# Down product of the last mixture from three products of rounded halves, transposes in pairs, result stored by groups

## The reference

```python
x = x + jnp.tanh(g_xattn[0]) * _L0_xattn_ref(_layernorm(x, axis=-1), ...)
x = x + jnp.tanh(g_ffn[0]) * _L0_ffn_ref(_layernorm(x, axis=-1), ...)
x = x + jnp.tanh(g_xattn[1]) * _L1_xattn_ref(_layernorm(x, axis=-1), ...)
x = x + jnp.tanh(g_ffn[1]) * _L1_ffn_ref(_layernorm(x, axis=-1), L1_ffn_gate_weight,
                                         L1_ffn_gate_up_weights, L1_ffn_down_weights,
                                         L1_ffn_shared_gate_up, L1_ffn_shared_down)
return x
```

## Time and profile before

| | us |
|---|---|
| median of 3 runs | 1322.51 |
| the three runs | 1320.82, 1322.51, 1324.74 |
| the profiled execution, its own time | 1319.32 |
| span of its trace | 1317.6 |
| busy PE, PEld, DVE, ACT, POOL | 1034.8, 852.9, 686.0, 431.5, 278.8 |
| last mixture, first product L1977 to last residual | 1003.3 to 1309.5 |

### The profile page before, as it was taken

The page is one execution under the profiler, slowest core; times in us unless marked ns, Lnnn a source line. Parts: engine busy times, 40 slices in busy tenths (PEclk is TensorE's granted clock), DMA queues, the critical chain, the costliest instruction groups (busy, mean ns, idle before and its releaser), DMA issues. The chain is left out here.

```text
span 1317.6 us, 16309 instructions
## 1 busy us (share of the span) xinstructions
PE 1034.8 (79%) x5307; PEld 852.9 (65%) x5307; DVE 686.0 (52%) x1618; ACT 431.5 (33%) x792; POOL 278.8 (21%) x225
## 2 busy tenths in 40 slices
PE   5989989989866502766566468797989999999997
PEld 3867858768655302656565236464668989898996
DVE  6277576675659895222223497556575324233221
ACT  4555455464624200111111042424252232322321
POOL 0414214133000002788787111010100000000000
PEclk9999999999886755788887676868667999899999
DMA  7004000000000141888886530000000000000001
GB/s 270 3 0 139 1 1 1 0 1 1 1 0 20 40 132 38 174 179 176 173 174 114 186 119 1 2 0 0 0 0 1 1 0 0 0 0 0 0 1 64
DMA packets 58887, 66.33 MB, mean 50 GB/s; under 512 B 5021, under 2 KB 55639, under 8 KB 58071
## 3 DMA queue, kind: packets, MB, share of 16 engines
q1 hardware_dynamic: 45188, 46.45, 11.3%
q0 software_dynamic: 12288, 18.88, 8.2%
q10 hardware_dynamic: 1363, 0.37, 0.1%
HBM read 48.13 MB, written 17.56 MB: 50 GB/s over the span
## 5 line engine op out<-in xcount | busy, mean ns | idle before, releaser
L1977 PE MATMUL bank<-gu_hi,xnT_split 128*128 128x352 f32 x640 | 158.7, 328 | 0.0
L474 POOL TENSOR_TENSOR q_lo<-soft,q_hi 128x512 fp32r<-128x512 f32 x64 | 93.3, 1458 | 236.1 <-ACT soft L1326 236.0
L1977 PEld LDWEIGHTS bank<-gu_hi,xnT_split 128*128 128x128 f32 x640 | 112.6, 190 | 1.0 <-issue 0.7
L495 POOL DMA_INDIRECT acc<-y,dst_now x64 | 102.3, 1598 | 26.3 <-issue 19.5
L485 POOL DMA_INDIRECT xg<-table,src_now x64 | 64.1, 1001 | 202.9 <-DVE src_now L940 183.7
L1977 PE MATMUL bank<-gu_lo,xnT_split 128*128 128x352 f32 x320 | 103.7, 324 | 0.0
L1196 DVE SCALAR_TENSOR_TENSOR soft<-sg,combine_w,bank 128x176 f32<-128x176 f32 x160 | 56.5, 395 | 87.6 <-PE bank L1977 81.8
L1996 PE MATMUL bank<-dn,attnT 128*128 128x256 f32 x448 | 101.8, 385 | 0.0
L1996 PEld LDWEIGHTS bank<-dn,attnT 128*128 128x128 f32 x448 | 85.9, 195 | 11.4
L713 DVE COPY qT<-bank 128x512 f32<-128x512 f32 x64 | 44.2, 691 | 87.4 <-PE bank L1675 86.3
L1528 ACT ACTIVATE sg<-bank 128x352 f32<-128x352 f32 x80 | 37.2, 465 | 152.0 <-PE bank L1977 151.9
(11 more groups left out here) (265 smaller groups left out, 2155.5 us busy)
## 6 DMA issues: line engine op xcount, KB each, us to landing
w_gu<-in_L_ffn_w_gu SPq DMA_DIRECT2D x32, 352.0 KB
w_dn<-in_L_ffn_w_down SPq DMA_DIRECT2D x32, 176.0 KB
acc<-zeros SPq DMA_DIRECT2D x2, 2176.0 KB, 11.4
acc_rows<-acc SPq DMA_DIRECT2D x8, 512.0 KB, 5.0
gu<-in_L_gu SPq DMA_DIRECT2D x1, 3520.0 KB, 13.8
table<-xw SPq DMA_DIRECT2D x4, 640.0 KB
wo<-in_L_xattn_Wo SPq DMA_DIRECT2D x2, 1024.0 KB, 16.0
wq<-in_L_xattn_Wq SPq DMA_DIRECT2D x1, 2048.0 KB, 18.3
```

The costliest lines, as they stand in the source:

```text
L474: pool.tensor_tensor(q2_lo[:, h % 3, :], q2[h % 2], q2_hi[:, h % 3, :], ALU.subtract).then_inc(q2_split, 1)
L495: pool.indirect_dma_start(acc[e], bass.IndirectOffsetOnAxis(ap=dst_now[:, q, e:e + 1], axis=0), y[:, q, e, :], None, compute_op=ALU.add).t ...
L1977: mm = pe.matmul(b[:, 0:2 * F1], v[:, c, j * P:(j + 1) * P], w[:, c, p, o, :], start=(n == 0), stop=(n == len(terms) - 1))
```

## The change

- The down weights are split once, in the first group, behind tile 0's silu and products: ACT rounds `dn1` to `dn_hi`, DVE subtracts to `dn_lo`, which lies on `dn1`. For this the first group is written out ahead of a loop over the two next.
- The transposes leave `down` and become `turn(j, groups)`. For tiles 0, 1 and 2 of a group they stand in the gates_ups of the next tile, two banks ahead of its third pair and two ahead of its fifth. For tile 3 all four banks stand ahead of down(3).
- ACT copies a turned bank rounded to `actT_hi`, and doesn't free it; DVE subtracts (`split_products`) to `actT_lo` and frees it. The last 96 rows of the 14th chunk are an instruction of their own.
- `down` does three products of fp32r for each chunk: hi x hi, hi x lo, lo x hi.
- ACT's exponential for the routing stands ahead of the copies of tile 3. PE waits, before the front, for the last turned bank.
- SP stores `x` in four transfers, one as soon as a group's four residuals are done.

```diff
@@ -224,7 +224,12 @@
-        dn1 = sb("dn1", [P, FC, DIM])
+        loaded = ExitStack()
+        dn1 = sb("dn1", [P, FC, DIM], scope=loaded)
+        loaded.close()
+        dn_lo = sb("dn_lo", [P, FC, DIM], F32R)
+        actT_hi = sb("actT_hi", [P, FC, P], F32R)
+        actT_lo = sb("actT_lo", [P, FC, P], F32R)
@@ -246,9 +251,12 @@
-        k_blocks = sb("k_blocks", [P, 2, C, 8, SKV])
-        v_blocks = sb("v_blocks", [P, 2, 2, 8, 2, D1])
-        c1 = sb("c1", [P, 2, DIM])
+        context = ExitStack()
+        k_blocks = sb("k_blocks", [P, 2, C, 8, SKV], scope=context)
+        v_blocks = sb("v_blocks", [P, 2, 2, 8, 2, D1], scope=context)
+        c1 = sb("c1", [P, 2, DIM], scope=context)
+        context.close()
+        dn_hi = sb("dn_hi", [P, FC, DIM], F32R)
@@ -444,9 +454,10 @@
-            sp.wait_ge(x_done, 1)
-            sp.dma_start(out_d, x[:]).then_inc(stored, 16)
-            sp.wait_ge(stored, 16)
+            for i in range(NG):
+                sp.wait_ge(o_read, 2 + 3 * NT + G * (i + 1))
+                sp.dma_start(out_d[:, G * i:G * (i + 1), :], x[:, G * i:G * (i + 1), :]).then_inc(stored, 16)
+            sp.wait_ge(stored, 16 * NG)
@@ -1068,6 +1079,15 @@
+            LAST = W1 - (FC - 1) * P
...
+            def split_down():
+                dve.wait_ge(dn_rounded, 1)
+                dve.tensor_tensor(dn_lo[:, 0:FC - 1], dn1[:, 0:FC - 1], dn_hi[:, 0:FC - 1], ALU.subtract).then_inc(
+                    dn_split, 1)
+                dve.tensor_tensor(dn_lo[0:LAST, FC - 1], dn1[0:LAST, FC - 1], dn_hi[0:LAST, FC - 1],
+                                  ALU.subtract).then_inc(dn_split, 1)
@@ -1171,7 +1191,7 @@
-                dve.wait_ge(t_ring.free, T5 + TMF - 8 + TM * i)
+                dve.wait_ge(t_ring.free, T5 + TMF - 4 + TM * i)
@@ -1186,9 +1206,25 @@
-            def products(i, j):
+            def split_products(i, j, groups):
...
+                for g in groups:
+                    n = min(4, FC - 4 * g)
+                    dve.wait_ge(act_rounded, 16 * i + 4 * j + g + 1)
+                    b = tr.read(dve)
+                    whole = n if g < 3 else n - 1
+                    ins = dve.tensor_tensor(actT_lo[:, 4 * g:4 * g + whole, :], b[:, 0:whole * P].rearrange(
+                        "p (f t) -> p f t", f=whole), actT_hi[:, 4 * g:4 * g + whole, :], ALU.subtract)
+                    if whole < n:
+                        ins = dve.tensor_tensor(actT_lo[0:LAST, FC - 1, :], b[0:LAST, whole * P:n * P],
+                                                actT_hi[0:LAST, FC - 1, :], ALU.subtract)
+                    ins.then_inc(t_ring.free, 1)
...
+            def products(i, j, before=None):
...
+                    if before is not None and p in (2, 4):
+                        split_products(i, before, (0, 1) if p == 2 else (2, 3))
@@ -1199,26 +1235,33 @@
+            tr = t_ring.end()
...
             def mixture(i, last):
...
                 qr.at(Q5, QM, i)
+                tr.at(T5 + TMF, TM, i)
                 products(i, 0)
+                if i is first_mixture:
+                    split_down()
                 if not last:
                     row_stats(i + 1)
-                products(i, 1)
+                products(i, 1, 0)
                 if not last:
...
                     row_apply(i + 1)
-                products(i, 2)
+                products(i, 2, 1)
                 residual(3 * NG + i, 1, i, 3)
-                products(i, 3)
-                if not last:
+                products(i, 3, 2)
+                if not last:
+                    tr.skip(TMF)
                     split_xn(i + 1)
...
                 residual(3 * NG + i, 2, i, 3)
+                split_products(i, 3, range(4))
                 residual(3 * NG + i, 3, i, 3)
@@ -1229,10 +1272,11 @@
             dve.wait_ge(o_read, 2 + 3 * NT)
-            with dve.Fori(0, NG - 1) as i:
+            first_mixture = 0
+            mixture(0, False)
+            with dve.Fori(1, NG - 1) as i:
                 mixture(i, False)
             mixture(NG - 1, True)
-            dve.drain().then_inc(x_done, 1)
@@ -1520,35 +1564,46 @@
-                def silu(j):
+                def silu(j, before=None):
                     for p in range(5):
+                        if before is not None and p in (2, 4):
+                            act_out(before, (0, 1) if p == 2 else (2, 3))
                         b = sr.read(act)
...
-                def act_out(j):
-                    for g in range(4):
+                def round_down():
+                    act.activation(dn_hi[:, 0:FC - 1], dn1[:, 0:FC - 1], ACT.Copy)
+                    act.activation(dn_hi[0:LAST, FC - 1], dn1[0:LAST, FC - 1], ACT.Copy).then_inc(dn_rounded, 1)
...
+                def act_out(j, groups):
+                    for g in groups:
                         n = min(4, FC - 4 * g)
-                        act.activation(attn_flat[:, 4 * g:4 * g + n, :], tr.read(act)[:, 0:n * P].rearrange(
-                            "p (f t) -> p f t", f=n), ACT.Copy).then_inc(t_ring.free, 1)
+                        b = tr.read(act)
+                        whole = n if g < 3 else n - 1
+                        ins = act.activation(actT_hi[:, 4 * g:4 * g + whole, :], b[:, 0:whole * P].rearrange(
+                            "p (f t) -> p f t", f=whole), ACT.Copy)
+                        if whole < n:
+                            ins = act.activation(actT_hi[0:LAST, FC - 1, :], b[0:LAST, whole * P:n * P], ACT.Copy)
+                        ins.then_inc(act_rounded, 1)
...
                 silu(0)
-                silu(1)
-                act_out(0)
-                silu(2)
-                act_out(1)
-                silu(3)
+                if i is first_mixture:
+                    round_down()
+                silu(1, 0)
+                silu(2, 1)
+                silu(3, 2)
                 if not last:
                     mixture_front()
-                act_out(2)
-                if not last:
                     gate_exponential(i + 1)
-                act_out(3)
...
-            attn_flat = attnT[:].rearrange("p b f t -> p (b f) t")
+                act_out(3, range(4))
...
+            LAST = W1 - (FC - 1) * P
             gate_exponential(0)
-            with act.Fori(0, NG - 1) as i:
+            first_mixture = 0
+            mixture(0, False)
+            with act.Fori(1, NG - 1) as i:
                 mixture(i, False)
@@ -1966,8 +2021,10 @@
-                def gates_ups(j):
+                def gates_ups(j, before=None):
                     for p in range(5):
+                        if before is not None and p in (2, 4):
+                            turn(before, (0, 1) if p == 2 else (2, 3))
                         for o, (ring, end) in enumerate(((s_ring, sr), (q_ring, qr))):
@@ -1978,40 +2035,52 @@
-                def down(j):
+                def turn(j, groups):
...
                     pe.wait_ge(q_ring.free, Q5 + QM * i + 5 * (j + 1))
-                    for g in range(4):
+                    for g in groups:
                         b = tr.fill(pe)
...
                         mm.then_inc(t_ring.full, 1)
+                    turned[j] = tr.k
...
+                turned = {}
...
+                def down(j):
...
                     pe.wait_ge(o_read, G * (3 * NG + i) + j + 1)
...
                         if f % 4 == 0:
-                            tr.evacuated(pe, 4 - f // 4)
-                        mm = pe.matmul(o_banks[j % 2][:, 0:DIM], attn_flat[0:n, f, :], dn1[0:n, f, :],
-                                       start=(f == 0), stop=(f == FC - 1))
+                            tr.evacuated(pe, tr.k - turned[j] + 4 - f // 4)
+                        for k, (v, w) in enumerate(((actT_hi, dn_hi), (actT_hi, dn_lo), (actT_lo, dn_hi))):
+                            mm = pe.matmul(o_banks[j % 2][:, 0:DIM], v[0:n, f, :], w[0:n, f, :],
+                                           start=(f == 0 and k == 0), stop=(f == FC - 1 and k == 2))
                     mm.then_inc(o_full, 1)
...
                 gates_ups(0)
-                gates_ups(1)
+                gates_ups(1, 0)
+                if i is first_mixture:
+                    pe.wait_ge(dn_split, 2)
                 down(0)
-                gates_ups(2)
+                gates_ups(2, 1)
                 down(1)
-                gates_ups(3)
-                if not last:
+                gates_ups(3, 2)
+                if not last:
+                    tr.evacuated(pe)
                     mixture_front(i + 1)
                 down(2)
+                turn(3, range(4))
                 down(3)
...
-            attn_flat = attnT[:].rearrange("p b f t -> p (b f) t")
+            first_mixture = 0
             pe.wait_ge(w_split, 5)
-            with pe.Fori(0, NG - 1) as i:
+            mixture(0, False)
+            with pe.Fori(1, NG - 1) as i:
                 mixture(i, False)
```

(4 more changed lines are left out.)

## The result

| | before | after |
|---|---|---|
| median, us | 1323.17 | 1301.74 |
| lowest and highest of 4 runs each | 1320.82, 1324.74 | 1300.55, 1303.27 |
| profiled execution, its own time / span | 1319.32 / 1317.6 | 1301.03 / 1299.1 |
| last mixture, first gates product to end of last residual | 1003.3 to 1309.5: 306.2 | 1004.1 to 1295.8: 291.7 |
| from there to the end of the span | 8.0 | 3.3 |

The account below looks back on a forecast made before the run. The prediction took TensorE's chain of sixteen tiles to bound the kernel; its terms, 14.6 + 5.0 - 3.6 + 0.5 - 4.5 - 2.0 + 4.0 = 14.0, taken from the 1322.5 median gave 1308.5 us, range 1302 to 1318.

Parts of the forecast that it names:

- 1 products: Down product per tile: 42 rounded products at 0.12 us, 5.04 against 5.95, winning 14.6 us over 16 tiles.
- 2 turning, tiles 0 to 2: Transposes placed in pairs among the next tile's products: 0.42 us of waiting for ACT goes in 12 tiles, 5.0 won.
- 3 turning, tile 3: Transposes ahead of down(3) wait for ACT's copy, then VectorE's subtraction: 0.9 us lost four times, -3.6.
- 4 changes of type: Late start after switching between f32 work and rounded products on TensorE: 3.0 us before, 2.5 after, +0.5.
- 5 split of the weights: First group, tile 1: TensorE waits for a bank while ACT and VectorE split the down weights, -4.5 us.
- 6 clock: Fronts' idle stays as it is; one more clock fall expected, partly inside the wait for the split weights, -2.0 us.
- 7 store: End of kernel: only the last 512 KB transfer remains, taken as 3.5 us where 2 MB took 7.5, +4.0.
- parts' good ends: The favourable bounds given for the parts' sizes; with every unknown at its good end the gain is about 20 us.
- the forecast's own case: The prediction's main case without the rivals: 1308.5 us, between 1303 and 1315, chance 0.78.
- The loads: Rival in the down product: weight loads space rounded products 0.19 us apart, 47 us more, 1355.5; chance 0.04.
- The clock does not fall at tile 3: Judges the rival that the clock falls in tile 3's bare transposes, costing 7 to 13.5 us, 1315.5 to 1322; chance 0.12.
- TensorE waits for VectorE: Rival: VectorE's subtractions delay freeing the up banks, 1.3 us in each of 12 tiles, 1324, no change; chance 0.06.

Follow-up runs that it names:

- the second comparison: The changed kernel run again with no edit, beside more runs of the kernel before: 1302.48 us against 1321.65, ratio 0.9858.
- the new order alone: The changed kernel with one f32 down product per chunk as before, ACT freeing the banks and no split of weights: 1312.48 us, ratio 0.9927.

## Why the prediction was short

By its own parts, with what the two profiles show in place of each:

| part | forecast | measured | from |
|---|---|---|---|
| 1 products | +14.6 | +13.6 | 16 x (5.87 - 5.02) |
| 2 turning, tiles 0 to 2 | +5.0 | +8.0 | 12 x (2.04 - 1.37) |
| 3 turning, tile 3 | -3.6 | -3.3 | 4 x (2.04 - 2.86) |
| 4 changes of type | +0.5 | +0.6 | 12 x (0.19 - 0.16), 4 x (0.19 - 0.08), less 3 x 0.08 |
| 5 split of the weights | -4.5 | -3.7 | idle at 1024.66 |
| 6 clock | -2.0 | 0.0 | 8.6 lost before, 8.6 after |
| 7 store | +4.0 | +4.7 | 8.0 - 3.3 |
| sum | 14.0 | 19.9 | |

In the table the change of type (0.19 before, 0.08 for each of the two pairs now) is taken out of the product and the turning; 2.86 is the mean of the four tiles 3 (2.81 to 2.93), from the start of the first transpose to that of the product. The profiles differ by 18.3, of which the stretch ahead of the mixture takes 0.8 back, so 19.1 stands against the 19.9 of the parts.

**Products: right in the new price, 1.0 too high in the gain.** 0.12 was taken, 0.1195 was measured. The f32 product was a little cheaper than the loads' starts suggested, 5.87 instead of 5.95. The price of a load alone, "0.122 each" for "eight loads" in 0.98, came from the same division as the step below; these loads start 0.111 to 0.112 apart (123.13 to 123.80). It did no harm here, because the rounded products of 256 columns gave 0.12 as well. The Trainium skill ("TensorE: Matmul & The Clock Gate", section "Back-to-back issue gap") gives 109 ns for 256 columns between isolated starts, and says itself that this under-counts a stream of loads and products with few columns; this trace has 119.5, so the formula is too low here at 256 columns as at 352, and the forecast was right not to sum by it.

**Turning in tiles 0 to 2: the step that failed.** The mechanism was right (the waits go), its size was not. The step is "Eight transposes load in 0.95, 0.12 each, so 14 of them are 1.68 and 0.42 of the 2.10 is waiting for ACT". A group's duration holds the tail of its last load. From the first start to the start of what follows, eight transposes are 0.79 and six 0.57, so fourteen are 1.37 (1.53 with the changes of type) and not 1.68, and what goes is 0.67 and not 0.42. That is 3.0 us over twelve tiles, and it was my error alone. The profile of before could have shown it: its transposes start 0.109 apart, and from the eighth of a tile (1293.42) to the ninth (1293.95) are 0.52.

**The clock: a term that cancelled.** The new fall came, 1.7 us, as forecast. But "The change leaves the fronts' idle as it is" was read as "the fronts cost the same", and they lost 6.9 instead of 8.6, so that the sum of both is nothing. The second profile of the same kernel lost 5.1 at its fronts. This looks like variation between executions and not like the change's work, and it was luck for the kernel; no forecast from one profile could have had it, and the range should have held some 3 us for it on either side.

**The split: right, 0.8 less.** ACT took 3.38 and VectorE 4.04 for what was put at 3.5 and 4.1, and the row statistics 1.9 for 2.15. So the wait ended at 1024.66, near the forecast's 1024.8, though the mixture started 0.8 later; TensorE came to it at 1020.98 instead of 1020.4.

**The store: right.** 2.9 us for 512 KB where 3.5 was taken, near the end that the write's own row gave.

**Tile 3: right.** The third bank was ready when the subtraction said, and 0.82 was lost where 0.9 stood.

**The base.** The median of before was 1322.5 in the first three runs and 1321.6 to 1321.8 in the later batches. The gain by later medians is 19.2, not 21.4. So of the 7 us between forecast and result some 5 are real, and the rest is in the runs. The bound of 1302, which was just missed, would have held the second median, 1302.48, so the side on which the first one fell is chance. That the gain is above 14.0 is not: the interval of the second comparison begins at 15.7. The parts' good ends add up to 20.9, which is 1301.6, and the forecast's own case was drawn down only to 1303. The 19.9 came by another way, with the products below their middle and the turning above its upper end of 5.

**The rivals.** The loads do not put the products 0.19 apart: they stand 0.1195 apart, and a fourth one costs about as much again, 0.115. The clock does not fall at tile 3, where the window has 1.00. The Trainium skill (same page, "Part 4: PE-mode transpose") says that transposes don't count as busy for the clock as products do; nothing here speaks for a fall from that, since in the experiment with the front pulled apart the logits and fourteen transposes around an idle of 1.0 stay at full clock too. In tiles 0 to 2 TensorE waits for VectorE at the split, and otherwise only about 0.1 us ahead of two fronts.

What stays open: where the mixture starts. It is at 1003.3 before, 1004.1 and 1003.9 in the two profiles of the changed kernel, and between 1004.0 and 1007.7 in the other experiments, though no edit changes what is computed ahead of it; with nothing changed but the store it is 1007.3. The traces narrow it down. At 730 us they are already up to 2.8 us apart. And in the two that start last (the store alone and the new order alone) TensorE stands at the lower level for 185 us between there and the mixture, in the nine others for 171 to 174. Why one execution has more of it is not shown.

## What to carry to other kernels

Take the price of a short TensorE instruction from start to start, never from the duration of a group divided by its count. A product made of three cheaper rounded ones paid here only with the new operands made beside other products: the same products with the transposes left in place gained nothing. And look at the idle of some two microseconds ahead of each stretch at low clock: pulling a front apart, which took 1.8 us of it away, was worth 4.

## What the hardware showed that I had not expected

The clock's falls went with the longer idles and not with the kind of work alone. Of 27 fronts with the idle of 1.8 us, in the nine profiles of kernels that have it, 24 were followed by a stretch at the lower level (1.2 GHz), of 3.4 or 6.8 us; of six fronts without it, in two kernels, none. The wait for the split weights, 3.7 or 4.6 us with rounded products on either side, was followed by one of 3.4 us in all six profiles that have it. An idle of 1.0 to 1.1 us at tile 3 was in no profile followed by one, nor were the nine more of that length that the kernel with the transposes in place has in its other tiles, away from the fronts. The length and the occurrence differ between executions of one kernel: the first front of the changed kernel fell in one profile and not in the other. All three fronts without a fall are first ones, whose idle is 1.72 us where the others have 1.79; but four other first fronts with 1.72 did fall, so this length doesn't settle it.
